# First weight loaded ahead of two cleared planes, and a first tile scored head by head

## The chip, the cores and the metric

The kernel runs on one core of one Trainium2 chip. The metric is the device time of one execution in microseconds (us). Before the change its median over three runs is 1173.93 us, from 1171.82 to 1175.15.

## The reference, cut to what matters

Two graph layers over 2048 nodes with 512 features. The first is an attention whose scores exist only for 10,000 listed pairs among the first 1500 nodes:

```python
q = (h[sub] @ Wq.T + bq).reshape(-1, 8, 64)      # h = relu(layernorm(x))
k = (h[obj] @ Wk.T + bk).reshape(-1, 8, 64)
att = (q * k).sum(-1) / sqrt(64)
scores = zeros(8, n, n).at[:, sub, obj].set(att)
scores = where(adj == 0, -inf, scores); diagonal = 1e-7
x = x + softmax(scores, axis=2).sum(0) / 8 @ h
```

The second is a graph attention with 16 heads over all nodes, with an output projection and an ELU. The change touches only the preparation and the first tile of the first layer.

## The kernel before, in words

**Stage 1** (`stage1`) normalises x in four quarters of four tiles, transposes Wk, Wq and the normalised tiles on TensorE (`turn`), and makes the projections q and k (`project`). TensorE's first work is the transposes of Wk. SP's queue issues the loads by hand in this order: the pair list, a clearing of plane 0, the first quarter of x, a clearing of plane 1, Wk, a clearing of plane 2, Wq, and the other three quarters of x.

**The planes** are three byte matrices of 1536 x 1536 in device memory, `rel_planes`, that together mark which pairs are listed. `scatter` on POOL (line 156) writes 80 batches of 125 marks, one indirect DMA each. `PLANE[e]` says which plane batch e goes to: planes 0, 0, 1, 2, 0, 1, 2 and so on. A batch waits for the clearing of its plane, or for the landing of the batch before it on the same plane. Ten batches come first, then five loads of adjacency tiles, each followed by four batches; the sixth and the seventh adjacency load stand ahead of batch 60 and batch 74 (`LATE_LOADS`, line 145). SP waits for all batches (line 573), then loads the first tile's rows of all planes. DVE joins them (`join_planes`, line 172), ANDs them with the adjacency (`mark_related`) and makes `low` (`first_low`), which each mask needs.

**Stage 2** makes the output tiles. In its front the order on every engine is written out by hand. TensorE gathers three unrelated tiles (line 691), projects the first (line 757), and makes the scores of the first related tile. `score(r, p)` makes the scores of heads 2p and 2p + 1 together: for each of three column chunks one matmul over the upper and one over the lower 64 rows of the array, into PSUM banks 0 to 2 and 3 to 5 (line 652). It waits until the two masks before are done. `score_head(r, hd)` makes one head with three matmuls and waits only for the mask that frees its own three banks; the kernel has it but does not call it. DVE masks head by head (line 1170), ACT takes the exponentials (line 956) and copies out transposed adjacency quarters (`copy_adj`, line 894), one of them (NU + 2, quarter 3) ahead of the exponentials of heads 6 and 7. After the last exponential ACT makes `edges`, and DVE's `factors` (from line 1137) starts the accumulation.

SP's loads of stage 2 begin when the projections are done (line 559): W_seq, two small vectors, three x tiles, and the stores of the adjacency chunks.

Of the kernel before, what the change touches and what calls it, by code (L numbers as in the profile page):

```python
# [39 lines left out]
EC = E // EP  # L40
PLANES = 3
# [20 lines left out]
ADJ_RING = 5  # L62
REL = 0x38
NU = NT - ET
PLANE = (0,) + tuple(i % PLANES for i in range(EC - 1))
LATE_LOADS = {60: ADJ_RING, 74: ADJ_RING + 1}


# [8 lines left out]
class FirstLayer:  # L77
# [69 lines left out]
    def scatter(self, pool, t, lo, hi):  # L147

        for e in range(lo, hi):
            plane = PLANE[e]  # L150
            n = PLANE[:e].count(plane)
            if n:
# [45 lines left out]
def stage1(nc, c, io, t, s, ps, f):  # L198
# [26 lines left out]
    Q, K = 0, 1  # L225
# [7 lines left out]
    def sync(sp):  # L233
        def load_x(i):
            sp.dma_start(h[:, CX * i:CX * (i + 1), :], io["x"][CX * P * i:CX * P * (i + 1), :]
                         .rearrange("(t p) k -> p t k", p=P)).then_inc(x_in[i], 16)

        def load_w(i, name):
            sp.dma_start(wnat[i][:, :, :], io[name].rearrange("(t p) k -> p t k", p=P)).then_inc(w_in[i], 16)
        sp.dma_start(rel[0:EP, :, :], io["L0_gnn_rel_pair_index"].rearrange("(p c) s -> p c s", p=EP)).then_inc(rel_in, 16)  # L240
        sp.wait_ge(zero_set, 1)
        f.clear_plane(sp, t, 0)
        load_x(0)
        f.clear_plane(sp, t, 1)
        load_w(K, "L0_gnn_Wk")
        f.clear_plane(sp, t, 2)
        load_w(Q, "L0_gnn_Wq")
        for i in range(1, 4):
            load_x(i)
# [159 lines left out]
    def tensor(pe):  # L409
# [34 lines left out]
        for j in range(NT):  # L444
            last = pe.matmul(ps[:, j // 4, j % 4 * P:(j % 4 + 1) * P], f.adjn[:, 0, j * P:(j + 1) * P], t["identb"][:, :],
                             start=True, stop=True)
            if j % 4 == 3:
                last.then_inc(adj_turned, 1)
        project(20, G, 20)
    return Programs(sync, gpsimd, vector, scalar, tensor)  # L450


# [19 lines left out]
def stage2(nc, c, io, t, s, ps, f, heads, begin):  # L472
# [5 lines left out]
    Q, K = 0, 1  # L478
# [49 lines left out]
    with nc.Block() as block:  # L528
        @block.sync
        def _(sp):  # L530
# [22 lines left out]
            def load_related(r):  # L553
                if r >= 2:
                    sp.wait_ge(f.marked, r - 1)
                f.load_related(sp, t, r)
# [15 lines left out]
            for i in range(PLANES):  # L572
                sp.wait_ge(f.related[i], 16 * PLANE.count(i))
            load_related(0)
# [65 lines left out]
        def _(pe):  # L640
            count = [0]

            def begin_round(*key):

                assert no[key] == count[0], (key, count)
                if count[0]:
                    pe.wait_ge(evicted, count[0])
                count[0] += 1

            def score_chunk(r, p, half, ch):  # L650
                rows, cols = slice(half * DK, (half + 1) * DK), slice(ch * 512, min(NREL, (ch + 1) * 512))
                return pe.matmul(ps[:, 3 * half + ch, 0:cols.stop - cols.start], qk[rows, Q, p, r * P:(r + 1) * P],  # L652
                                 qk[rows, K, p, cols], start=True, stop=True)

            def score(r, p):

                if r or p:
                    pe.wait_ge(masked, HA * r + 2 * p)
                for ch in range(CH):
                    for half in range(2):  # L660
                        last = score_chunk(r, p, half, ch)
                        if ch == CH - 1:
                            last.then_inc(scores, 1)

            def score_head(r, hd):

                pe.wait_ge(masked, HA * r + hd - 1)
                for ch in range(CH):
                    last = score_chunk(r, hd // 2, hd % 2, ch)
                last.then_inc(scores, 1)  # L670

            def turn_adj(k, q):
                begin_round("adj", k, q)
                if q == 0:
                    pe.wait_ge(f.adj_in[k % ADJ_RING], 16 * (k // ADJ_RING + 1))
                for i in range(4):
                    j = 4 * q + i
                    last = pe.matmul(ps[:, 6, i * P:(i + 1) * P], adjn[:, k % ADJ_RING, j * P:(j + 1) * P],
                                     t["identb"][:, :], start=True, stop=True)
                last.then_inc(written, 1)  # L680

            def gather(u, piece):

                if piece == 0 and u:
                    pe.wait_ge(based, u)
                if piece == 0:
                    pe.wait_ge(*((evicted, no["adj", u, 3] + 1) if u else (f.chunk0_ready, 4)))
                for i in range(6 * piece, 6 * piece + 6):
                    j, part = i // 3, i % 3
                    moving = (f.upper(h[:, j, :]), f.upper(f.rest[:, j, :]), f.tail[:, j, :])[part]  # L690
                    last = pe.matmul(ps[:, 7, :], chunk[place(u)][:, j, :], moving, start=(i == 0), stop=(i == 3 * NT - 1))
                if piece == 7:
                    last.then_inc(agg, 1)
# [11 lines left out]
            def turn(r, m):  # L705
                for b in range(2):
                    last = pe.transpose(ps[:, 6, b * P:(b + 1) * P],  # L707
                                        W[r % 2][:, (2 * m + b) * P:(2 * m + b + 1) * P], t["ident"][:, :])
                return last
# [9 lines left out]
            def turn_one_and_scores(n):  # L719

                begin_round("one", n)
                if 1 <= n < ET:
                    turn(n - 1, 1)
                if n < 0:
                    pe.wait_ge(w12_ready, 2 * KT)
                for k in range(KT):
                    last = pe.matmul(ps[:, 6, 2 * P:2 * P + 2 * HB], h2T[:, k, :], w12[:, k, :], start=(k == 0), stop=(k == KT - 1))
                last.then_inc(written, 1)
# [19 lines left out]
            def turn_h(k):  # L748
                begin_round("h", k)
                pe.wait_ge(h2_ready, k + 1)  # L750
                for b in range(KT):
                    last = pe.transpose(ps[:, 6, b * P:(b + 1) * P], h2[:, b * P:(b + 1) * P], t["ident"][:, :])
                last.then_inc(written, 1)
# [7 lines left out]
            def project(k):  # L761
                begin_round("proj", k)
                if k == 0:
                    pe.wait_ge(wseq_in, 16)
                project_part(k, 0, KT)

            def front():
                begin.tensor(pe)
                pe.wait_ge(f.biased_out, GROUPS)
                pe.wait_ge(f.parted, 2 * NT)  # L770
                for i in range(8):
                    gather(0, i)
                    turn_adj(NU if i % 2 else 1, i // 2)
                for i in range(8):
                    gather(1, i)
                    turn_adj(3 if i % 2 else 2, i // 2)
                turn_h(0)
                score(0, 0)
                for i in range(8):
                    gather(2, i)  # L780
                    if i % 2:
                        turn_adj(NU + 1, i // 2)
                project(0)
                score(0, 1)
                turn_one_and_scores(-1)
                turn_h(1)
                turn_adj(NU + 2, 0)
                score(0, 2)
                turn_adj(NU + 2, 1)
                score(0, 3)  # L790
                for q in (2, 3):
                    turn_adj(NU + 2, q)

            def step(n):
# [46 lines left out]
            def last_steps():  # L841
# [37 lines left out]
                heads.spread_top(pe)  # L879
                project_part(ET + 3, 2, KT)  # L880
            front()
            for n in range(ET - 1):
                step(n)
# [901 lines left out]
```

## Time and profile before

| | us |
|---|---|
| median of three runs | 1173.93 |
| the profiled execution | 1171.58 |
| its span | 1169.6 |
| PE busy | 1091.6 (93%) |
| DVE busy | 950.2 (81%) |
| ACT busy | 807.5 (69%) |
| POOL busy | 121.7 (10%) |

The span goes from the first to the last instruction; 1.98 us lie around it. The profiled execution is 2.35 us below the median. In the busy tenths of the page, PE is idle in the first slice, drops to 6 in one slice in the first fifth and to 5 in one past the middle, and is otherwise at 9. Views of the trace used here are the timeline (start, duration, engine, line, operation, count, and in brackets the idle time before and what ended it), the chain of work that ended last, and busy times by stretch.

### The profile page before, as it was taken

How to read it: one execution, taken by the hardware profiler on the slowest of the kernel's cores; microseconds unless marked ns; L12 is line 12 of the kernel's file. 1: busy time of each engine (PE TensorE's matmuls, PEld its weight loads, DVE VectorE, ACT ScalarE, POOL GpSimd, SP SyncE). 2: the span in 40 equal slices, each digit the busy share in tenths (PEclk: the TensorE clock that was granted, in tenths of full speed). 3: DMA queues.
4: the chain of work that ended last, by engine and by line, in shares of the span. 5: the costliest groups of instructions: out<-in, count | busy, mean ns of one | idle time of the engine just before them, and what ended most of it. 6: DMA issues, size and time to landing. Idle time of an engine off the chain costs nothing.

```text
span 1169.6 us, 24648 instructions
## 1 busy us (share of the span) xinstructions
PE 1091.6 (93%) x10565; PEld 756.0 (65%) x10565; DVE 950.2 (81%) x1325; ACT 807.5 (69%) x843; POOL 121.7 (10%) x140
## 2 busy tenths in 40 slices
PE   1999986999999999999995999999999999999997
PEld 1444433444444444444443999999999999999743
DVE  2355336999999999998826899999999999999565
ACT  1334327677777777776426999999999999998122
POOL 2778640000000000000000000000000000000011
PEclk9999998999999999999998999999999999999999
DMA  9630453222222111100433101001111011111311
GB/s 340 145 23 2 110 104 88 55 65 57 66 66 66 45 41 46 37 28 27 162 126 130 39 38 38 38 38 38 39 38 38 38 38 38 38 39 38 109 72 72
DMA packets 38269, 77.69 MB, mean 66 GB/s; under 512 B 5653, under 2 KB 15250, under 8 KB 36114
## 3 DMA queue, kind: packets, MB, share of 16 engines
q1 hardware_dynamic: 31954, 67.62, 16.1%
q0 software_dynamic: 6208, 8.50, 6.0%
q8 instruction: 84, 1.38, 0.5%
q14 instruction: 23, 0.19, 0.1%
HBM read 65.39 MB, written 23.21 MB: 76 GB/s over the span
## 4 chain that ended last, share of the span: by engine, by line
PE 60%; DVE 9%; issue 9%; ACT 7%; DMA 1%; DVEq 0%; POOL 0%; SPq 0%
PE psum L1587 14%; PE psum L1584 8%; PE psum L1585 8%; PE psum L1588 8%; PE psum L737 7%; PE psum L652 7%; PE psum L1682 5%; DVE area_b L1170 3%; DVE f_region L1159 3%; ACT area_b L956 2%; ACT f_region L943 2%; ACT area_h L1431 2%; PE psum L707 1%; PE psum L757 1%; PE psum L1673 1%
## 5 line engine op out<-in xcount | busy, mean ns | idle before, releaser
L1431 ACT ACTIVATE area_h<-area_a,keep 128x2048 fp8e4<-128x2048 f32 x208 | 397.0, 1989 | 2.3 <-DMA area_a<-s_rows 2.3
L1587 PE MATMUL psum<-s_V,area_h 128*128 128x198 bf16 x2048 | 285.9, 248 | 0.0
L1588 PE MATMUL psum<-s_V,late 128*128 128x99 bf16 x2048 | 279.9, 208 | 0.0
L1584 PE MATMUL psum<-s_V,area_h 128*128 128x99 bf16 x2048 | 206.0, 210 | 12.1 <-DVE area_b L1486 11.3
L1585 PE MATMUL psum<-s_V,area_b 128*128 128x99 bf16 x2048 | 205.9, 209 | 0.0
L1587 PEld LDWEIGHTS psum<-s_V,area_h 128*128 128x128 fp8e4 x2048 | 199.6, 97 | 0.1
L1588 PEld LDWEIGHTS psum<-s_V,late 128*128 128x128 fp8e4 x2048 | 199.5, 97 | 0.0
L1584 PEld LDWEIGHTS psum<-s_V,area_h 128*128 128x128 fp8e4 x2048 | 189.5, 98 | 13.5 <-issue 12.4
L1585 PEld LDWEIGHTS psum<-s_V,area_b 128*128 128x128 fp8e4 x2048 | 189.6, 98 | 0.0
L737 PE MATMUL psum<-area_h,f_region 128*128 128x512 f32 x384 | 184.9, 596 | 0.0
L1481 DVE TENSOR_TENSOR area_h<-area_h,area_a 128x512 uint32<-128x512 uint32 x256 | 171.2, 684 | 11.3 <-ACT area_h L1431 6.9
L1159 DVE SCALAR_TENSOR_TENSOR f_region<-area_b,s_r,f_region 128x1500 f32<-128x1500 f32 x96 | 170.8, 1780 | 2.2
L1170 DVE CUSTOM_DVE_ANT_0 area_b<-psum,late 128x1500 f32<-128x1500 f32 x96 | 161.1, 1715 | 7.2 <-PE psum L652 7.0
L956 ACT ACTIVATE area_b<-area_b,s_negm 128x1500 f32<-128x1500 f32 x96 | 147.8, 1540 | 23.9 <-DVE s_negm L1170 22.9
L652 PE MATMUL psum<-area_a 64*128 64x512 f32 (+1 forms) x576 | 138.6, 615 | 13.2 <-DVE s_negm L1170 13.1
L156 POOL DMA_INDIRECT rel_planes<-f_ones,f_flat x80 | 99.5, 1244 | 56.1 <-DMA rel_planes<-f_ones,f_flat 21.0
L652 PEld LDWEIGHTS psum<-area_a 64*128 64x128 f32 x576 | 53.4, 192 | 72.8 <-issue 49.8
L737 PEld LDWEIGHTS psum<-area_h,f_region 128*128 128x128 f32 x384 | 65.0, 191 | 43.0 <-issue 43.0
L902 ACT ACTIVATE f_region<-psum 128x256 f32<-128x256 f32 x96 | 36.6, 381 | 79.5 <-PE psum L707 63.9
L431 PE MATMUL psum<-f_region 128*128 128x512 f32 x192 | 83.7, 594 | 5.0 <-DVE f_region L304 3.8
L1486 DVE TENSOR_TENSOR area_b<-area_a,area_h 128x512 uint32<-128x512 uint32 x128 | 87.4, 683 | 0.0
L431 PEld LDWEIGHTS psum<-f_region 128*128 128x128 f32 x192 | 36.1, 190 | 49.5 <-issue 43.3
(171 smaller groups left out, 1155.9 us busy)
## 6 DMA issues: line engine op xcount, KB each, us to landing
area_a<-s_rows SPq DMA_DIRECT2D x16, 1024.0 KB, 4.7
rel_planes<-f_h SPq DMA_DIRECT2D x3, 2304.0 KB, 16.0
late<-rel_planes SPq DMA_DIRECT2D x36, 192.0 KB, 2.7
area_h<-in_x SPq DMA_DIRECT2D x4, 1024.0 KB, 12.9
keep<-in_adj POOLq DMA_DIRECT2D x16, 256.0 KB, 6.3
f_region<-in_x SPq DMA_DIRECT2D x16, 256.0 KB, 4.7
x<-f_region SPq DMA_DIRECT2D x16, 256.0 KB, 2.0
area_a<-adj_chunks SPq DMA_DIRECT2D x4, 1024.0 KB, 9.2
```

The source lines that it names most:

```text
L431: last = pe.matmul(ps[:, 4 + g % 4, :], wT[w][:, k, dt * P:(dt + 1) * P], hT[:, k, ch * 512:(ch + 1) * 512], start=(k == 0), stop=(k == KT ...
L652: return pe.matmul(ps[:, 3 * half + ch, 0:cols.stop - cols.start], qk[rows, Q, p, r * P:(r + 1) * P], qk[rows, K, p, cols], start=True, st ...
L737: last = pe.matmul(ps[:, 7 if r < ET - 1 else 0, :], WT[m % 2][:, b, :], h[:, 2 * m + b, :], start=(m == order[0] and b == 0), stop=(m == ...
L956: act.activation(ex[:, hd, 0:NREL], ex[:, hd, 0:NREL], ACT.Exp, bias=negm[:, b, hd:hd + 1], scale=-1.0, accum_out=zs[:, b, hd:hd + 1]).the ...
L1159: dve.scalar_tensor_tensor(w, ex[:, hd, 0:NREL], r8[:, hd:hd + 1], w, ALU.mult, ALU.add).then_inc(added if hd < HA - 1 else w_ready, 1)
L1170: dve.tensor_tensor_reduce(ex[:, hd, 0:NREL], ps[:, 3 * (hd % 2):3 * (hd % 2) + 3, :].rearrange("p c j -> p (c j)")[:, 0:NREL], low[r % 2] ...
L1431: act.activation(masks[:, j, :], s1b[:, b, :], ACT.Relu, bias=t["s2"][:, n, 0, j:j + 1], scale=BIG, saturate=False).then_inc(signs, 1)
L1481: dve.tensor_tensor(own, own, adjT[:, :, j, :].bitcast(U32), ALU.bitwise_and).then_inc(mask_ready, 1)
L1584: pe.matmul(out[:, :, 0:DZ], masks[:, j, cols], V[:, b, j, :, 0:DZ], **first)
L1585: last = pe.matmul(out[:, :, DZ:CZ], fars[:, FAR.index(j), cols], V[:, b, j, :, DZ:CZ], **then)
L1587: pe.matmul(out, masks[:, j, cols], V[:, b, j, :, :], **first)
L1588: last = pe.matmul(out[:, :, DZ:CZ], nadjT[:, NEAR_TILES.index(j), cols], V[:, b, j, :, DZ:CZ], **then)
```

## The change

Wk is issued right behind the first quarter of x, ahead of the clearing of plane 1; planes 1 and 2 are then cleared one after the other. The batches are distributed anew: 0, 0, 0, then 1, 0 three times, then 1, 2, 0, 1, 2, 0 and so on, so that plane 2 is first used by batch 10. In TensorE's front the pair calls for heads 2 to 7 become six calls of `score_head`, and the transposes of adjacency tile NU + 2 stand one behind each of the last four.

```diff
-PLANE = (0,) + tuple(i % PLANES for i in range(EC - 1))
+PLANE = (0, 0, 0) + (1, 0) * 3 + tuple((i + 1) % PLANES for i in range(EC - 9))
@@
         load_x(0)
+        load_w(K, "L0_gnn_Wk")
         f.clear_plane(sp, t, 1)
-        load_w(K, "L0_gnn_Wk")
         f.clear_plane(sp, t, 2)
@@
                 project(0)
-                score(0, 1)
+                score_head(0, 2)
                 turn_one_and_scores(-1)
+                score_head(0, 3)
                 turn_h(1)
-                turn_adj(NU + 2, 0)
-                score(0, 2)
-                turn_adj(NU + 2, 1)
-                score(0, 3)
-                for q in (2, 3):
+                for q in range(4):
+                    score_head(0, 4 + q)
                     turn_adj(NU + 2, q)
```

## Rows read from the trace of the kernel before

**Rows 1.** Page: the span.
```profile
span 1169.6 us, 24648 instructions
```

**Rows 2.** Chain that ended last: start us, us, what. Its beginning and the first tile's end.
```profile
173.68 0.12 DVE area_b L1170
...
197.97 0.49 ACT f_region L894
198.46 3.05 ACT area_b L956 x4
...
201.92 0.24 DVE s_z L1137
```

**Rows 3.** Timeline, DVE: the first x quarter, and the first join of planes.
```profile
14.03 2.47 DVE L285 BATCH_NORM_STATS2 s_stats<-area_h 128x6 f32<-128x512 f32 x4 [9.98 <-DMA area_h<-in_x]
...
170.18 1.15 DVE L172 TENSOR_TENSOR late<-late 128x384 uint32<-128x384 uint32 x2 [17.81 <-DMA late<-rel_planes]
```

**Rows 4.** Timeline, PE: its first work, and the first related tile's scores.
```profile
22.68 3.65 PE L421 MATMUL psum<-ident,late 128*128 128x128 f32 x16 [22.68 <-DMA late<-in_L_gnn_Wk]
...
169.56 3.70 PE L757 MATMUL psum<-f_region,f_h2T 128*128 128x512 f32 x8 [0.69 <-ACT f_region L894]
177.10 4.48 PE L652 MATMUL psum<-area_a 64*128 64x512 f32 x12 [3.84 <-DVE s_negm L1170]
181.51 1.08 PE L727 MATMUL psum<-s_w,f_h2T 128*128 128x32 f32 x8
182.91 0.65 PE L752 MATMUL psum<-ident,f_h 128*128 128x128 f32 x4 [0.32 <-ACT scores L909]
184.25 0.40 PE L678 MATMUL psum<-identb,keep 128*128 128x128 bf16 x4 [0.69 <-ACT f_h2T L936]
185.04 2.79 PE L652 MATMUL psum<-area_a 64*128 64x512 f32 x12 [0.39 <-DVE s_negm L1170]
```

**Rows 5.** Timeline, POOL: batches 0, 1, 2, 3, 6, 9 and 13.
```profile
12.13 1.25 POOL L156 DMA_INDIRECT rel_planes<-f_ones,f_flat  x1 [7.69 <-DMA rel_planes<-f_h]
18.80 1.22 POOL L156 DMA_INDIRECT rel_planes<-f_ones,f_flat  x1 [5.42 <-DMA rel_planes<-f_ones,f_flat]
20.38 1.19 POOL L156 DMA_INDIRECT rel_planes<-f_ones,f_flat  x1 [0.36 <-DMA rel_planes<-f_h]
28.93 1.18 POOL L156 DMA_INDIRECT rel_planes<-f_ones,f_flat  x1 [7.36 <-DMA rel_planes<-f_h]
...
34.52 1.19 POOL L156 DMA_INDIRECT rel_planes<-f_ones,f_flat  x1 [1.43 <-DMA rel_planes<-f_ones,f_flat]
...
39.77 1.18 POOL L156 DMA_INDIRECT rel_planes<-f_ones,f_flat  x1 [0.89 <-DMA rel_planes<-f_ones,f_flat]
...
46.92 1.18 POOL L156 DMA_INDIRECT rel_planes<-f_ones,f_flat  x1 [0.83 <-DMA rel_planes<-f_ones,f_flat]
```

**Rows 6.** Timeline, POOL: batch 59, the sixth adjacency load, batches 62, 63 and 77.
```profile
123.00 1.19 POOL L156 DMA_INDIRECT rel_planes<-f_ones,f_flat  x1 [0.30 <-issue]
124.18 0.62 POOL L145 DMA_DIRECT2D keep<-in_adj  x1
...
130.44 1.18 POOL L156 DMA_INDIRECT rel_planes<-f_ones,f_flat  x1 [2.62 <-DMA rel_planes<-f_ones,f_flat]
134.06 1.18 POOL L156 DMA_INDIRECT rel_planes<-f_ones,f_flat  x1 [2.44 <-DMA rel_planes<-f_ones,f_flat]
...
160.20 1.19 POOL L156 DMA_INDIRECT rel_planes<-f_ones,f_flat  x1 [3.42 <-DMA rel_planes<-f_ones,f_flat]
```

**Rows 7.** Timeline, SP's queue: W_seq, and the load of x tile 3.
```profile
123.24 0.37 SPq L559 DMA_DIRECT2D f_region<-in_L_gnn_W_seq  x1
...
152.06 0.33 SPq L536 DMA_DIRECT2D f_region<-in_x  x1
```

**Rows 8.** Stretches: us, length, busy of PE, PEld, DVE, ACT, POOL; clock, DMA share, GB/s.
```profile
38.00:40.00 2.00, 2.00 (x6) 0.95 (x5) 0.00 (x0) 0.00 (x0) 1.11 (x2) 1.00 0.22 43
...
178.00:180.00 2.00, 2.00 (x8) 0.99 (x6) 1.37 (x3) 1.09 (x2) 0.00 (x0) 0.50 0.43 131
```

## The prediction

> **What bounds the kernel now.** I read the page first: PE is busy 93% of a span of 1169.6 us [rows 1], so a gain has to come from a stretch where PE waits. The chain of waits says which. Its traced part begins at 173.68 us with the mask of head 0 of the first related tile [rows 2]; from there it runs through masks and scores of that tile and, later, mostly through PE. So everything ahead of 173.68 counts only through what releases that mask. Two chains run up to it, and I then followed each in the timeline of its engines.
>
> Chain A is stage 1 and PE. PE starts at 22.68, released by the landing of Wk, although the first quarter of x was there at 14.03 [rows 3, 4]. It ends in the projection at 169.56, 3.70 us long, so at about 173.3 [rows 4].
>
> Chain B is the scatter. Eighty batches leave POOL one behind another: 1.19 us and 0.30 us of issue, 1.49 together [rows 6]. DVE sat idle 17.81 us until the plane rows had landed, joined them at 170.18, and masked at 173.68 [rows 2, 3]. The mask needs `low`, which hangs on B alone; the gathering of tile 2, its other condition, is over before the projection of 169.56. A and B arrive together by chance: A is what the next scores need, B what the mask needs.
>
> **Part 1, Wk ahead of plane 1.** Wk landed 2.30 us behind plane 1 (22.68 against POOL's start on plane 1 at 20.38, [rows 4, 5]), so 2.3 us is what its 1 MB takes. Behind the first quarter of x it should land near 14.0 + 2.3 = 16.3. The four norms, 14.03 to about 20.7, then overlap Wk's transposes, and the last copy of a turned x tile ends about as far behind PE's start as now. A gains 22.7 - 16.5 = 6.2 us, at most 8.6 if Wk landed with x. Nothing later in A takes it back: Wq, the other quarters and the adjacency loads keep their places in front of needs that have slack. A then ends near 167. But this gain is not in the sum: PE reaches the scores of head 2 six microseconds earlier and waits for the mask. Its price would be zero even if Wk came no earlier, since A was not what released the mask. Moving it delays plane 1 from about 20.4 to 22.7, and leaves plane 2 at 28.9, as the same bytes stand ahead of it.
>
> **Part 2, the batches.** What a batch takes to land follows from the batch that waited for it. Batch 0 left at 12.13 and batch 1 at 18.80, less 0.3 of start-up: 6.4 us. Batch 3 to 6: 28.93 to 34.52, so 5.3. Batch 6 to 9: 34.52 to 39.77, so 4.95 [rows 5]. With three planes in turn a landing may take 4.2 us before POOL waits, with two only 2.7. Walked through with 5.5 us: batch 1 at 18.8, 2 at 24.6, 3 (plane 1) at 26.1, 4 at 30.4, 5 at 31.9, 6 at 36.2, 7 at 37.7. The heavy traffic ends about there (43 GB/s between 38 and 40, [rows 8]), so batch 8 goes at about 40 and batch 9 at 41.5, against 39.77: 1.7 us later. With 5.0 us it is 1.6, with 6.4 us 3.9. I take +1.8. All five adjacency loads behind it slip too, but their readers come tens of microseconds later. From batch 10 on three planes take turns again, and an adjacency load ahead of the batch costs what it does now (batch 13 idle 0.83 rather than 0.30, [rows 5]).
>
> Two larger stalls lie further on. Between batch 59 (123.00) and batch 63 (134.06) pass 11.06 us, against 4 x 1.49 + 0.62 = 6.58 for four batches and a load: 4.5 us lost [rows 6]. Batch 77 lost 3.42 - 0.30 = 3.1 [rows 6]. In both an adjacency load of POOL's queue met a burst from SP's (W_seq and x tiles from 123.24, x and chunk tiles around 152.06, [rows 7]). The bursts belong to A and come 6.2 us earlier, at 117 and 146; the adjacency loads stay where B is. So they come apart. The early burst alone still holds up a batch: batch 59 took 130.44 - 0.3 - 123.00 = 7.1 us to land, 2.9 beyond the free 4.2. I put 2.3 for it and 1.8 for the adjacency load behind it, together 4.1 instead of 4.5; and for the second place 0.8 + 0.55 (the load alone, as at batch 13) instead of 3.1. That is -0.4 and -1.8. Ends: all stay as they are (0), or both pairs shrink to loads alone (-6.4). B: +1.8 - 0.4 - 1.8 = -0.4, between +3.9 and -4.
>
> **Part 3, head by head.** Now six column matmuls of two heads run as 12 passes in 2.79 us at full clock, 0.23 each, since the two halves of the array work at once. Right after PE's idle 3.84 us the same took 4.48, with a granted clock of 0.50, the 1.2 GHz level, between 178 and 180; idling costs 1.69 us [rows 4, 8]. A single head is not in the trace. Bounds: 1.40 (half a pair) and 2.79 (as long as a pair). The nearest row for matmuls that don't share the array is the projection, 8 full-height passes of 512 columns in 3.70, of which about 0.43 is the pace of one; six are 2.6. I take 2.6, so each pair costs 2.4 us of PE more, 7.2 in all.
>
> The Trainium skill, "TensorE: Matmul & The Clock Gate", Part 3: Packing small matmuls, says that a matmul over few rows takes as long as one over all rows, and that the gain comes from several running at once in different rows. By this rule the change gives the pairing away and a head costs what I took; if a head cost half a pair, the time would be that of the second rival below. No run here shows a single head yet.
>
> In exchange a head starts one mask earlier and PE no longer stands still. In us behind the first mask's start (173.68 before): first mask done 1.78; head 2 from a cold clock 2.6 + 1.7, to 6.05; the small products 0.95 (line 727) to 7.0; head 3 to 9.6; turning h 0.65 to 10.3; heads 4 to 7 with an adjacency quarter of 0.40 behind each, 4 x 3.0, to 22.3 [rows 4]. Masks of 1.7 follow each head and, from head 4 on, keep pace; DVE's unrelated tile, the join and the marking of tile 1 fit between. ACT copies the last quarter (0.49) and does the exponentials of heads 6 and 7 (3.05), to 25.9; with 0.4 for `edges` the factors start at 26.4. Before: 201.92 - 173.68 = 28.2 [rows 2]. Gain 1.8 us. The new wait: that last copy stands ahead of ACT's exponentials of heads 6 and 7 and now comes behind head 7, so no exponential of head 6 runs under it.
>
> **Sum.** B -0.4, front -1.8: -2.2 us. Behind it DVE, then PE, are the bound, and pass the shift on. Profiled execution 1171.58 - 2.2 = 1169.4. It stands 2.35 under the median of the three runs; against the median the forecast is 1171.7.
>
> **Rivals.**
> - *The bursts and the loads come fully apart.* For it: both big stalls lie where two queues met. Against it: 7.1 us of landing began ahead of the adjacency load. Then B is 1.8 - 4.5 + 0.5 - 3.1 + 0.5 = -4.8, which I cut to -3 for what a burst alone must cost; with the front -4.8, 1169.1.
> - *Single heads cost half a pair.* Then PE is done with the heads long before ACT; ACT's own list (exponentials 1.54 each, count, copies) ends near 23.2, another 3.2 us saved: 1168.5.
> - *No gain in the front.* If eviction waits of some tenths at each of the four quarters, or 2.8 instead of 2.6 per head, eat the 1.8: -0.4, 1173.5.
> - *Slower: landings of 7 us in the two-plane stretch.* Batch 0's took 6.4 in like traffic, so 7 is near. Walked through, batch 4 goes at 33.6 and batch 9 at 44.5, +4.7; the end of the traffic near 38 caps it there. If the late stalls stay as they are, B is +4.7 and the whole +2.9: 1176.8. It decides from about +1.8 in B, a landing of 5.5 with no late saving.
> - *The change doesn't do what it says:* A's six microseconds reach the end. This needs the mask to hang on A, and 17.81 us of DVE idleness ended by the plane rows speak against it.
>
> **How the numbers follow.** Forecast 0.50, stalls gone 0.20, half-price heads 0.05, no front gain 0.13, long landings 0.12; the last rival under 0.01. A measurement tells about 0.3%, 3.5 us, from no change. Faster than that: most of the stalls-gone and half-price cases and a tail of the forecast, 0.28. Slower: a tail of long landings, 0.06. Within: 0.66. The range leaves out the ends of the bounds: 1167.5 to 1176.
>
> **What would show it.** PE's first matmul near 16.5 and its projection ending near 167, then an idle 6 to 8 us of PE ahead of line 652. Batch 9 near 41.5, the last batch between 160 and 167. The first mask between 171 and 176. Six groups of six passes of line 652, 2.6 us each, the first about 4.3. Factors 26.4 us behind the first mask. The prediction is wrong if the mask starts by more than 3 us elsewhere than 173.3, if heads cost 1.4, or if a steady step later in the kernel changes its length.

## Result: slower by 1.1%, and where the profile after shows it

The changed kernel takes 1184.39 us (median of 4 runs, 1181.7 to 1187.99) against 1172.88 for the kernel before in the same comparison: ratio 1.0112, 95% interval 1.008 to 1.0145. The forecast was 1171.7 with a range up to 1176, so the prediction was wrong, in size and in sign. The profiled execution took 1186.9 us with this span:

```profile
span 1185.0 us, 24648 instructions
```

That is 15.4 us more than [rows 1]. Two instants split it: the first mask of the first related tile, and the start of its factors. From the timeline of DVE after the change (as in [rows 3], and to be held against [rows 2]):

```profile
171.41 1.15 DVE L172 TENSOR_TENSOR late<-late 128x384 uint32<-128x384 uint32 x2 [22.47 <-DMA late<-rel_planes]
...
174.91 1.72 DVE L1168 CUSTOM_DVE_ANT_0 area_b<-psum,late 128x1500 f32<-128x1500 f32 x1
...
217.69 0.23 DVE L1135 SCALAR_TENSOR_TENSOR s_z<-s_e,s_n,s_zs 128x8 f32<-128x8 f32 x1 [1.72 <-ACT s_e L961]
```

The mask starts 1.2 us later than the 173.68 of before. From there to the factors it takes 42.8 us instead of 28.2, so 14.5 us are lost between these two; with the 1.2 ahead of them that is 15.8, and some 0.4 come back behind the factors. The timeline of PE shows in what (line 652 is a head's scores, six passes; the lines of before are [rows 4]):

```profile
166.07 3.70 PE L757 MATMUL psum<-f_region,f_h2T 128*128 128x512 f32 x8 [0.69 <-ACT f_region L892]
176.69 5.37 PE L652 MATMUL psum<-area_a 64*128 64x512 f32 x6 [6.92 <-DVE s_negm L1168]
181.98 1.91 PE L727 MATMUL psum<-s_w,f_h2T 128*128 128x32 f32 x8
183.83 5.37 PE L652 MATMUL psum<-area_a 64*128 64x512 f32 x6
189.12 1.11 PE L752 MATMUL psum<-ident,f_h 128*128 128x128 f32 x4
190.17 5.37 PE L652 MATMUL psum<-area_a 64*128 64x512 f32 x6
195.47 0.61 PE L678 MATMUL psum<-identb,keep 128*128 128x128 bf16 x4
196.01 5.36 PE L652 MATMUL psum<-area_a 64*128 64x512 f32 x6
...
214.86 5.37 PE L652 MATMUL psum<-area_a 64*128 64x512 f32 x12 [1.28 <-DVE s_negm L1168]
220.16 3.87 PE L757 MATMUL psum<-f_region,f_h2T 128*128 128x512 f32 x8
```

Every single head takes 5.37 us, twice 2.7, and every other operation between the heads is slow too: 1.91 for 1.08, 1.11 for 0.65. At 214.86 a pair, with twice the passes, takes the same 5.37. The stretches (columns as in [rows 8]; the number behind the counts of POOL is the granted clock) show the reason:

```profile
178.00:180.00 2.00, 2.00 (x3) 0.70 (x3) 1.93 (x5) 2.00 (x4) 0.00 (x0) 0.50 0.27 26
...
200.00:202.00 2.00, 2.00 (x7) 0.51 (x5) 0.59 (x1) 0.05 (x1) 0.00 (x0) 0.50 0.00 0
...
222.00:224.00 2.00, 2.00 (x6) 0.88 (x5) 1.97 (x2) 1.00 (x3) 0.00 (x0) 1.00 0.96 120
```

From 176.69 to 213.58 us, 36.9 us long, PE is busy without a break, and yet the clock stays at 0.50, the 1.2 GHz level. It had fallen while PE idled ahead of head 2 (0.69 between 172 and 174, 0.50 from 174 on), and it comes back to 1.00 only behind the first pair of the next tile (0.86 between 220 and 222). In the chain that ended last the six heads now stand one behind another, here the third and fourth of them:

```profile
190.24 5.30 PE psum L652 x6
195.53 0.54 PE psum L678 x4
196.08 5.29 PE psum L652 x6
```

### The profile page after: what moved, and what is told of

The parts are those of the page before. It is cut to its first block, busy times and chain, and to the rows that moved or that the text cites. A ratio compares the mean times of both kernels' runs of the same rounds, so it can differ in the third digit from the quotient of the medians.

```text
span 1185.0 us, 24648 instructions
## 1 busy us (share of the span) xinstructions
PE 1116.8 (94%) x10565; PEld 765.9 (65%) x10565; DVE 950.6 (80%) x1325; ACT 808.1 (68%) x843; POOL 121.6 (10%) x140
## 4 chain that ended last, share of the span: by engine, by line
PE 61%; DVE 8%; issue 8%; ACT 7%; DMA 1%; DVEq 0%; POOL 0%; SPq 0%
PE psum L1585 14%; PE psum L652 8%; PE psum L1582 8%; PE psum L1583 8%; PE psum L1586 8%; PE psum L737 7%; PE psum L1680 5%; DVE f_region L1157 3%; DVE area_b L1168 3%; ACT area_b L954 2%; ACT f_region L941 2%; ACT area_h L1429 2%; PE psum L707 1%; PE psum L757 1%; PE psum L678 1%
## 5 line engine op out<-in xcount | busy, mean ns | idle before, releaser
L652 PE MATMUL psum<-area_a 64*128 64x512 f32 (+1 forms) x576 | 161.4, 640 | 11.6 <-DVE s_negm L1168 11.6
L954 ACT ACTIVATE area_b<-area_b,s_negm 128x1500 f32<-128x1500 f32 x96 | 147.8, 1540 | 26.4 <-DVE s_negm L1168 25.3
L652 PEld LDWEIGHTS psum<-area_a 64*128 64x128 f32 x576 | 60.7, 200 | 80.7 <-issue 59.7
```

What stands on the lines that cost most here:

```text
L954: act.activation(ex[:, hd, 0:NREL], ex[:, hd, 0:NREL], ACT.Exp, bias=negm[:, b, hd:hd + 1], scale=-1.0, accum_out=zs[:, b, hd:hd + 1]).the ...
```

## Experiments

My theory after this reading: single heads, which use 64 of the array's 128 rows, do not bring the clock up after an idle stretch, whereas in the traces before and after the change it rose again under or behind a pair. Rivals: the longer idle stretch ahead of head 2, made by Wk's new place; and the single stream of matmuls as such, whatever its height. In all fences below, PE rows are from the timeline of the kernel named, stretches from its busy times by stretch. A ratio is the time over that of the kernel before in the same comparison, with its 95% interval.

**One part at a time.** First the new order without the single heads.

```diff
 # changed kernel, TensorE's front
-                score_head(0, 2)   # and heads 3 to 7
+                score(0, 1)        # and pairs 2 and 3, as before
```

> The changed kernel with the first tile's scores in pairs again, so the new order of Wk and the planes alone. Theory (the single heads are the loss): the first mask comes at about 174.9 us as in the changed kernel, 1.2 later than before, and from there to the factors it takes 28.2 us as before instead of 42.8; span about 1170.8, 14 us under the changed kernel, line 652 back to 2.8 us a pair when warm and 4.4 after an idle stretch. Rival (the longer idle of PE ahead of the first score is the loss, whatever follows): the pairs too stay at a granted clock of 0.50 up to the factors, 5.4 us each, and the span stays above 1178.

Measured: 1172.02 us (10 runs), ratio 1.0007, 0.9984 to 1.0031. First mask at 174.75, factors at 204.03, 29.3 us apart, span 1169.8. PE idled longer than in the changed kernel ahead of the first scores, and the pairs brought the clock up all the same (a pair wholly at 0.50 takes 5.37 us, wholly at 1.00 it takes 2.79):

```profile
178.17 4.23 PE L652 MATMUL psum<-area_a 64*128 64x512 f32 x12 [10.45 <-DVE s_negm L1170]
...
185.86 2.79 PE L652 MATMUL psum<-area_a 64*128 64x512 f32 x12 [0.40 <-DVE s_negm L1170]
...
192.10 5.37 PE L652 MATMUL psum<-area_a 64*128 64x512 f32 x12 [2.74 <-DVE s_negm L1170]
```

So the idle stretch alone is not it, and the new order by itself costs nothing that can be measured. Then the single heads without the new order:

```diff
 # kernel before, TensorE's front
-                score(0, 1)        # and pairs 2 and 3
+                score_head(0, 2)   # and heads 3 to 7, as in the changed kernel
```

> The kernel before with the first tile's scores head by head, Wk and planes as before. Theory: the heads alone carry the loss: each takes 5.4 us at a granted clock of 0.50, factors about 43 us behind the first mask, span 1169.6 + 14.5 = 1184. Rival (it needs the 6.9 us of idle that Wk's new place makes): PE idles only some 2 us ahead of head 2, the clock holds at 1.00 and the heads take 2.6 us each; span about 1168.

Measured: 1184.12 us (4 runs), ratio 1.0117, 1.006 to 1.0174; first mask 172.54, factors 213.29, 40.8 us apart. All of the loss is in this part. The rival's condition was met, PE idled only 1.18 us and came in at 1.00 (the stretch from 174 to 176); but the clock fell under head 2 (0.60 between 176 and 178) and stayed down to the first pair of the next tile:

```profile
174.32 3.33 PE L652 MATMUL psum<-area_a 64*128 64x512 f32 x6 [1.18 <-DVE s_negm L1168]
177.58 1.92 PE L727 MATMUL psum<-s_w,f_h2T 128*128 128x32 f32 x8
179.42 5.37 PE L652 MATMUL psum<-area_a 64*128 64x512 f32 x6
```

**Height.** The same number of matmuls and columns, over all rows. Each score then holds the neighbouring head's products too, so this kernel's result is not the right one; it serves the clock alone.

```diff
 # changed kernel, in score_head
-                    last = score_chunk(r, hd // 2, hd % 2, ch)
+                    cols = slice(ch * 512, min(NREL, (ch + 1) * 512))
+                    last = pe.matmul(ps[:, 3 * (hd % 2) + ch, 0:cols.stop - cols.start],
+                                     qk[:, Q, hd // 2, r * P:(r + 1) * P], qk[:, K, hd // 2, cols], start=True, stop=True)
```

> The changed kernel in which each of heads 2 to 7 of the first tile is scored with all 128 rows instead of its own 64, with the same number of matmuls, columns and waits; it thus adds the neighbouring head's products to each score. Theory (height is what the clock goes by): the first head is part cold, about 4.3 us, the others 2.6 at a granted clock of 1.00; span about 1169 to 1171. Rival (number or spacing of the matmuls, their single stream): 5.4 us each as in the changed kernel, 1185.

Measured: 1167.99 us (10 runs), ratio 0.9961, 0.9939 to 0.9983. PE idled 8.44 us, the first head ran at 0.50 throughout, the second at 1.00 (the last line is the next tile's pair, to be compared further below):

```profile
175.49 5.37 PE L670 MATMUL psum<-area_a 128*128 128x512 f32 x6 [8.44 <-DVE s_negm L1170]
...
181.92 2.76 PE L670 MATMUL psum<-area_a 128*128 128x512 f32 x6
...
197.94 2.79 PE L652 MATMUL psum<-area_a 64*128 64x512 f32 x12 [1.60 <-DVE s_negm L1170]
```

First mask 173.70, factors 200.59: 26.9 us, where the prediction had 26.4. Against the changed kernel only the height differs, and it is worth 16 us. The rival of the single stream falls.

**Does half height also bring the clock down?** Here PE is kept at work ahead of head 2 by making the first projection three times:

```diff
 # changed kernel, in project, for k == 0, ahead of the projection itself
+                    for _ in range(2):
+                        for b in range(KT):
+                            pe.matmul(ps[:, 6, :], h2T[:, b, :], wseq[:, b, :], start=(b == 0), stop=(b == KT - 1))
```

> The changed kernel with the four matmuls of the first projection made three times over, so that PE works at full height until about 176.8 us and comes to head 2 warm. Theory A (half-height matmuls cannot raise the clock but do not lower it): 2.6 us a head throughout, factors 26.4 us behind the first mask, which is 16 us less; span about 1169. Theory B (half-height matmuls alone count as little, so the clock also falls under them): the first heads take 2.6 us, then 5.4; span 1176 to 1183. Theory C (a fixed cost of single heads whatever the clock): 5.4 us each from the first on, 1185.

Measured: a median of 1168.83 us over 10 runs, which says little: seven lie between 1167.4 and 1169.3, three between 1180.8 and 1183.6. The mean granted clock over the span, measured in every execution, goes with it: 0.988 to 0.991 in the seven, 0.975 to 0.978 in the three. The difference of some 0.013 over 1170 us is about 30 us at half the clock, so in the seven the clock held under most or all of the heads. The profile is of one of the three (span 1181.7):

```profile
170.73 3.60 PE L757 MATMUL psum<-f_region,f_h2T 128*128 128x512 f32 x8
175.62 3.27 PE L652 MATMUL psum<-area_a 64*128 64x512 f32 x6 [1.29 <-DVE s_negm L1171]
178.82 1.91 PE L727 MATMUL psum<-s_w,f_h2T 128*128 128x32 f32 x8
180.66 5.37 PE L652 MATMUL psum<-area_a 64*128 64x512 f32 x6
```

The same kernel once more, for a profile of the group near 1168:

> The kernel with the first projection made three times over, once more, for a profile of an execution in which the clock holds (7 of 10 times were near 1168 us, 3 near 1182). If the profile is of the fast group: granted clock 1.00 from 164 us on, single half-height heads of 2.8 us each from line 652 with an idle stretch of 1.3 us ahead as in the slow one; so the same gap ends either way. If the gap is shorter than 1 us here, the gap's length decides and not chance.

It gave 1184.72 us, again the longer time, with an idle stretch of 2.01 us. So no trace shows how long PE idled in the seven. One more making of the projection closes the gap:

```diff
-                    for _ in range(2):
+                    for _ in range(3):
```

> The changed kernel with the first projection made four times over, so that PE is still busy at full height when the first mask is done (end near 177.9 us) and goes into head 2 without the 1.3 us of idling of the run with three. There 7 of 10 executions took about 1168 us and 3 about 1182. Theory 1 (the idle gap makes the clock fall): now all executions are fast, about 1170 (the projection ends some 2 us after the mask). Theory 2 (half-height work alone can let the clock fall): slow ones at about 1183 are still among them, with the heads at 5.4 us.

Measured: 1170.67 us (10 runs, 1168.56 to 1174.22), ratio 0.9991, 0.9973 to 1.0009; no time near 1182, and the mean granted clock of every execution is 0.988 or more. The extra work ended after the first mask, so the time is not a gain; what counts is the clock, 1.00 under all single heads:

```profile
179.31 2.78 PE L652 MATMUL psum<-area_a 64*128 64x512 f32 x6
...
195.44 2.78 PE L652 MATMUL psum<-area_a 64*128 64x512 f32 x6
200.04 5.37 PE L652 MATMUL psum<-area_a 64*128 64x512 f32 x12 [1.49 <-DVE s_negm L1171]
```

The same without extra work, the first two heads being a pair:

```diff
 # changed kernel, TensorE's front; heads 4 to 7 stay single
-                score_head(0, 2)
+                score(0, 1)
                 turn_one_and_scores(-1)
-                score_head(0, 3)
```

> The changed kernel with heads 2 and 3 of the first tile made as a pair and only heads 4 to 7 one by one. The pair brings the clock up as in the kernel before, so this asks what half-height matmuls do to a clock that is up, without extra work ahead. Theory 1 (half-height matmuls cannot raise the clock; a clock that is up stays as long as PE is busy): heads 4 to 7 take 2.6 us each in all executions, factors about 26 us behind the first mask, span about 1168. Theory 2 (half-height work by itself lets the clock fall, and in some executions it does so sooner than in others): among heads 4 to 7 it falls from 1.00 to 0.50 in the profile, and the times spread over more than 5 us or sit near 1175 to 1180.

Measured: 1168.4 us (10 runs, 1165.29 to 1172.83), ratio 0.9976, 0.996 to 0.9991. The pair came in at 0.50 behind 6.80 us of idling and brought the clock up; the four single heads behind it kept it:

```profile
174.66 4.64 PE L652 MATMUL psum<-area_a 64*128 64x512 f32 x12 [6.80 <-DVE s_negm L1167]
...
181.21 2.78 PE L652 MATMUL psum<-area_a 64*128 64x512 f32 x6
184.25 2.78 PE L652 MATMUL psum<-area_a 64*128 64x512 f32 x6
...
194.93 4.48 PE L652 MATMUL psum<-area_a 64*128 64x512 f32 x12 [1.49 <-DVE s_negm L1167]
```

```profile
184.00:188.00 4.00, 4.00 (x16) 1.88 (x17) 3.65 (x5) 3.94 (x7) 0.00 (x0) 1.00 0.01 4
188.00:192.00 4.00, 4.00 (x13) 1.65 (x13) 2.52 (x4) 4.00 (x6) 0.00 (x0) 1.00 0.01 2
```

Theory 1 holds, then, with one addition. Single half-height heads never raised the clock in any trace. Without an idle stretch ahead of them they kept it: in both traces (the pair first leaves 0.31 us of idling shortly ahead of them), and by their times in all 20 executions of these two kernels, where the kernel with an idle stretch had three long ones in ten. With a stretch of 1.2 to 2.0 us ahead, the clock fell under them in each of the three executions profiled, which are all of the longer kind.

Even where the clock held, the half-height heads left something behind. The pair of the next tile, behind 1.49 us of idling, took 5.37 us after six of them and 4.48 after four, so it ran at 0.50 wholly or in part. After six full-height heads the same pair, behind 1.60 us, took 2.79 (the last line of the full-height run).

**The batches.** POOL's timeline after the change shows batches 2, 3, 4, 8 and 9, to be read against [rows 5]:

```profile
23.51 1.19 POOL L156 DMA_INDIRECT rel_planes<-f_ones,f_flat  x1 [4.87 <-DMA rel_planes<-f_ones,f_flat]
25.01 1.19 POOL L156 DMA_INDIRECT rel_planes<-f_ones,f_flat  x1 [0.30 <-issue]
29.74 1.19 POOL L156 DMA_INDIRECT rel_planes<-f_ones,f_flat  x1 [3.55 <-DMA rel_planes<-f_ones,f_flat]
...
40.09 1.19 POOL L156 DMA_INDIRECT rel_planes<-f_ones,f_flat  x1 [1.84 <-DMA rel_planes<-f_ones,f_flat]
41.58 1.19 POOL L156 DMA_INDIRECT rel_planes<-f_ones,f_flat  x1 [0.30 <-issue]
```

Batch 9 leaves at 41.58 where the prediction's walk gave 41.5. To see what the alternation of two planes costs, only one batch more than before is put on plane 0:

```diff
 # the kernel with pairs and Wk first
-PLANE = (0, 0, 0) + (1, 0) * 3 + tuple((i + 1) % PLANES for i in range(EC - 9))
+PLANE = (0, 0) + tuple(i % PLANES for i in range(EC - 2))
```

> Pairs again, Wk first again, and the batches as 0, 0, 0, 1, 2, 0, 1, 2 and so on: only one more batch on plane 0 before plane 2 is clear, no stretch that alternates between two planes. Theory (the alternation costs what batch 9 lost, 2 us): batch 9 leaves near 38 us instead of 41.6 to 41.9, the first mask comes near 172 instead of 174.8, span about 1167.5 against 1169.8 of the run with pairs. Rival (the bursts further on set the end whatever the start): the first mask still comes at 174 to 175 and the time is that of the run with pairs.

Measured: 1169.89 us (10 runs), ratio 0.9973, 0.9961 to 0.9984. Batch 9 left at 37.87 and the first mask started at 170.04, 4.7 us ahead of the run with pairs. But the time is only some 0.3% better, since the factors came at 202.16, just 1.9 us ahead. The 2.8 us between are PE's: the first two pairs ran at 0.50 for longer than in the run with pairs, 5.37 and 4.48 us against 4.23 and 2.79, although the idle stretches ahead of them were no longer, 5.61 and 0.30 us against 10.45 and 0.40. Why the clock came back later here, no run separates.

```profile
173.47 5.37 PE L652 MATMUL psum<-area_a 64*128 64x512 f32 x12 [5.61 <-DVE s_negm L1170]
...
182.29 4.48 PE L652 MATMUL psum<-area_a 64*128 64x512 f32 x12 [0.30 <-DVE s_negm L1170]
...
190.23 5.37 PE L652 MATMUL psum<-area_a 64*128 64x512 f32 x12 [3.13 <-DVE s_negm L1170]
```

**Versions that beat both kernels.** Two of the things learned, put together: this order of batches, Wk first, one pair, then four single heads.

```diff
 # the kernel with the pair first
-PLANE = (0, 0, 0) + (1, 0) * 3 + tuple((i + 1) % PLANES for i in range(EC - 9))
+PLANE = (0, 0) + tuple(i % PLANES for i in range(EC - 2))
```

> Wk first, batches 0, 0, 0, 1, 2, 0, 1, 2 and so on, the first pair of heads as a pair, heads 4 to 7 one by one; no extra work. The two parts were measured apart: the batches bring the first mask 2 to 4 us forward, the pair ahead of four single heads takes 26 to 27 us from the first mask to the factors, against 28 to 29 with pairs only. If they add: first mask near 171, factors near 197.5, time 1166. If the bursts eat the batches' gain again: as e5, 1168.4.

Measured: 1164.74 us (10 runs, 1163.81 to 1168.37), ratio 0.9944, 0.9927 to 0.996. First mask 169.93, factors 196.59, 26.7 us apart: the parts add. The four single heads behind the pair take 2.78 us each again, and the next tile's pair, behind 1.49 us, again 4.48. The other way is height, with the right result. DVE spreads q once into a zeroed tile, 1.7 us of work in a place where it otherwise idles for some 20 us:

```diff
 # changed kernel with the batches as above; DVE, ahead of its first unrelated tile
+                dve.wait_ge(f.biased_out, GROUPS)
+                dve.memset(W[0][:, 0:6 * P], 0.0).then_inc(padded, 1)
+                dve.wait_ge(padded, 1)
+                for s in range(2):
+                    rows = slice(s * DK, (s + 1) * DK)
+                    dve.tensor_copy(qpad[rows, :, s, :], qk[rows, Q, 1:4, 0:P]).then_inc(padded, 1)
 # left out here: score_head waits for padded; stationary qpad[:, hd // 2 - 1, hd % 2, :], moving qk[:, K, hd // 2, cols]
 # left out here: the first projection is made twice
```

> Head by head at full height with the right result: q of heads 2 to 7 of the first tile is copied once into a tile whose other 64 rows are zero, so each matmul runs over 128 rows. With the batches of the last run and the first projection made twice, so that PE idles little ahead of head 2. Theory (height of the matmul, zeros or not, is what the clock goes by): granted clock 1.00 through all heads, 2.6 to 2.8 us each, factors 24.5 us behind the first mask, first mask near 172, span about 1164. Rival (zero rows count as no work): clock 0.50 and 5.4 us a head, span about 1180, or two groups of times as with three projections.

Measured: 1163.69 us (4 runs), ratio 0.9923, 0.9906 to 0.994. First mask 170.26, factors 194.21, 24.0 us apart. Behind 1.28 us of idling zero-padded heads kept the clock:

```profile
172.14 2.75 PE L674 MATMUL psum<-area_a,f_region 128*128 128x512 f32 x6 [1.28 <-DVE s_negm L1177]
175.54 2.76 PE L674 MATMUL psum<-area_a,f_region 128*128 128x512 f32 x6
```

In the profiled execution of the kernel with three projections half-height heads lost it behind 1.29 us. But in seven of that kernel's ten executions the clock held too, so four here do not tell the two apart. Whether padded heads bring the clock up does; it was asked by leaving the second projection away:

> The padded kernel without the second making of the first projection, so PE idles several us ahead of head 2 and comes to it at the 1.2 GHz level. Theory (height brings the clock up, zeros or not): the first head 5.4 us at a granted clock of 0.50, the rest 2.7 at 1.00, as in the run with full-height heads and the neighbour's products; factors near 26.9 us behind the first mask, 3 us more than the padded run, time near 1166.5. Rival (zeros count as no work, and the padded run was fast only because it came in warm): the heads stay at 5.4 us, 1180.

Measured: 1165.63 us (7 runs), ratio 0.9944, 0.9926 to 0.9961. The first head ran at 0.50, the second at 1.00; factors 26.5 us behind the mask of 170.98.

```profile
172.85 5.34 PE L674 MATMUL psum<-area_a,f_region 128*128 128x512 f32 x6 [5.57 <-DVE s_negm L1174]
...
178.84 2.76 PE L674 MATMUL psum<-area_a,f_region 128*128 128x512 f32 x6
```

So rows that hold zeros count like any others here. The second projection is worth 2.5 us in this stretch; between 1163.7 and 1165.6 us in all, from different comparisons, I would not rank the two too firmly.

## Why the prediction was wrong, by its own steps

**Bound.** Right. The mask hung on chain B, and A's gain was not in the end time. PE's first matmul came at 17.43 rather than near 16.5, and its projection ended at 169.8 rather than 167 in the profile after; in the runs with pairs, with the pair first and at full height it ended between 167.0 and 167.9. In all of them PE then idled between 6.8 and 10.5 us. The run with pairs shows that this part alone leaves the time as it was.

**Batches.** The walk to batch 9 held (41.58 for 41.5). The total, -0.4 us, came out as +1.2 in the profile after. SP's burst came 5.0 us earlier (W_seq at 118.22 for 123.24), and by POOL's rows the first of the two late stalls was mis-sized: from batch 55 to batch 64 pass 19.74 us against 18.55, so 1.2 more, where I had 0.4 less. The second gave 2.1 us back (batch 64 to 79 in 25.49 us against 27.60), where I had 1.8. Seven profiled executions have these batches, and their first mask starts anywhere between 171.24 and 174.91, mean 173.9; the kernel before has 173.68 and, with single heads, 172.54. A forecast to a few tenths was finer than executions repeat. That the alternation of two planes was the costly part is shown by the four with the other order: 169.93 to 170.98, mean 170.3, which is 3.6 us earlier; batch 9 alone is 3.7 us earlier (37.87 for 41.58).

**Head by head: the step that failed.** It was the line "head 2 from a cold clock 2.6 + 1.7, to 6.05", and the 2.6 of each head after it. The 1.7 was the pair's row at the low clock less its row at the high one [rows 4]. I carried it over to a single head, and took for granted that busy PE time of any kind ends the low clock. With six heads of 5.3 instead of 4.3 + 5 x 2.6 that term is short by 14.5 us; the small products, the turning of h and the adjacency quarters, all at half clock, add about 1.8 (0.9, 0.4 and four times 0.14 from start to start). Together 16.3, against 42.8 - 26.4 = 16.4 measured. The rest of the step was sound, but for a slip of 0.1 us (25.9 + 0.4 is 26.3). At the high clock a single head takes 2.78 us from start to end, and the schedule of 26.4 us is what full height gave (26.9).

The price of a head at full clock was a good one, and here the rule quoted ahead bore out. The Trainium skill, "TensorE: Matmul & The Clock Gate", has a matmul over few rows take as long as one over all; the rule stands in its section "Why this matters for your kernels", not in Part 3, which describes the packing. The trace agrees, 2.78 us for six passes over 64 rows and 2.76 over 128. Part 1 of the same page of the Trainium skill describes the clock as coming up behind sustained work of PE. By that alone the changed kernel would have come back to 1.00 under its single heads; the 36.9 us of unbroken work at 0.50 from 176.69 on disagree, and the measurement decides.

**Rivals.** Half-price heads, no front gain, long landings and vanished stalls all ended within 5.5 us of the kernel before. None was a clock that stays low, although its ingredients stood in the rows: an idle stretch ahead, a granted clock of 0.50 behind it, and work unlike any whose effect on the clock the trace showed. At 5.4 us a head the same sum would have given 1171.58 - 0.4 + 14.6, about 1186, where the profile has 1186.9. That was the rival on the slow side to put forward, in place of landings of 7 us.

**What stays open.** Why the kernel with three projections falls into two groups of times (7 of 10, 3 of 10): both profiles are of the longer kind. Whether idling of less than 1.18 us ahead of single heads is harmless: it was at most 0.3 us or at least that. And where between 64 and 128 rows the clock begins to rise: no run used a height between them.

## What to carry to other kernels

A matmul that uses half the rows costs its own time and, behind an idle stretch, possibly the clock of all that follows it: look in the trace for a stretch where just such work stands alone and read the granted clock there, before pricing it from rows at the high level. If scores must be made one by one, put a pair first with no idle stretch behind it, or pad with zeros. And where a mask or wait moves ahead by some microseconds, read the granted clock of the stretch behind it again: of the 4.7 us that the other order of batches brought, 2.8 went back as time at 0.50.

## What the runs showed of the hardware that I had not expected

- Single heads of six passes over 64 rows, PE busy all the time from 176.69 to 213.58 us: granted clock 0.50 throughout, and on to 220 us, until the next tile's pair and projection. Over 128 rows: 5.37 us for the first head and 2.76 for the next.
- Zeros in the other 64 rows do as well as data: 5.34, then 2.76 us.
- A clock at 1.00 survived four to six single heads with no gap ahead (2.78 us each), and fell under them behind gaps of 1.18, 1.29 and 2.01 us; by the times it also held in seven of ten executions of the kernel that showed the 1.29.
- A pair behind 1.5 us of idling took 4.48 to 5.37 us after half-height heads (three traces), and 2.79 us behind 1.6 us after full-height ones, zeros or not (three traces).
- A batch of 125 one-byte writes amid other traffic of about 400 GB/s (the stretches from 14 to 36 us) takes about 6 us to land (batch 2 left 6.1 us after batch 1, at 23.51, held up by its landing), so two planes in turn leave POOL idle up to 3.6 us at a time (batch 4).
